# Causal masking without mask products: a fused maximum on VectorE and zeroed exponentials on GpSimd, with later sums and projections

## The chip, the cores and the metric

One core of a Trainium2 chip runs the whole program. The metric is the device time of one execution in microseconds (us); less is better. The core has five engines with a queue each: TensorE (PE in the profile), VectorE (DVE), ScalarE (ACT), GpSimd (POOL), and SyncE (SP), which issues DMAs. They meet only through semaphores.

## The reference, cut to what matters

The model looks up token vectors (16 sequences of 512, width 128), mixes them once with a low-rank attention, and then runs a block with routed experts and an MLP. The change is in the block's three attentions, 8 heads of width 16 over 512 tokens each. Spatial (S) and cross (C) attention see all keys, temporal (T) attention is causal:

```python
logits = jnp.einsum('bthd,bshd->bhts', q, k) * HD ** (-0.5)
causal = jnp.tril(jnp.ones((T, T), dtype=bool))
logits = jnp.where(causal, logits, -jnp.inf)
att = jax.nn.softmax(logits, axis=-1)
o = jnp.einsum('bhts,bshd->bthd', att, v).reshape(B, T, D)
```

## The kernel before, in words

There are three stages, one after the other: `embed_and_mix`, `attend`, `feed_forward`. The change touches `attend` alone, which computes for each of the 16 sequences three units, S, T and C.

A unit passes through PE twice. First the scores are computed with queries on the partitions, only to find each query's maximum: 32 tiles (8 heads x 4 blocks of 128 queries), `score` (line 1114), each reduced by VectorE in `reduce` (919). The negated maxima are split into three bf16 rows and stacked under the queries (`negate`, 927). Then the scores are computed again, keys on the partitions, with the maximum already subtracted: 32 tiles, `logits` (1129), each taken through Exp by ScalarE into `probs` (`exponential`, 1026). Four tiles make a group; `weigh` (1144) multiplies a group with the values and sums over the keys: 8 sums per unit, of which the first four belong to the first half of the heads. For T, only the causal part of a tile is computed, 128 to 512 columns, and each tile of both passes gets one more product of 128 columns that adds -1e30 above the diagonal: lines 1125 and 1140, `ident_bf` times `mask_row` or `mask_col`.

q, k and v come from fp32 projections into one PSUM bank, the desk (`project`, 1084). ScalarE keeps q and k; GpSimd splits them in bf16 parts (`split`, 841), SyncE stacks the parts by DMA (`stack`, 794).

The order is written out by hand. The loop runs over i, each with three slots of 32 tiles. In a slot, four units are at work (`units`, 731): `kn` is projected and split, `ka` is scored, `kb` is in its second pass (its first 24 tiles), `ko` ends (its last 8 tiles, the last sums, the merges and the output). Slot 0: kn = T, ka = S, kb = C, ko = T. Slot 1: kn = C, ka = T, kb = S, ko = C. Slot 2: kn = S, ka = C, kb = T, ko = S. At tile n, PE does score n, what falls due at n (the projections at PROJECT_AT, in desk order), logit n - 8, and a sum where n % 4 is 3. The others follow the same count: ScalarE keeps q and k at KEPT_AT, copies the second group of sums (`s_high`, `u_high`) at tile 12 and the first (`s_all`, `u_all`) at tile 28, and makes the reciprocal at 21 (a logarithm and an exponential); VectorE adds the value bias at VALUES_AT and shuffles the merged sums at SWAP_AT, 17 (`swap`, 962), after waiting for GpSimd's merge (line 870).

GpSimd's own queue in a slot (863): split q and k of `kn`, merge `s_all` (870) and `u_all` (871) of `ko`, an affine or a bias in some slots, the product with the reciprocal (889), and in slots 1 and 2 the affine for a later unit.

Two rings limit how far the engines run apart. There are three PSUM banks for scores, so score n waits until reduction n - 3 is done, and three for logits, so logit n waits for exponential n - 3. `probs` has two buffers, one group each, so the exponentials of group q wait for sum q - 2. The sums of all groups share one bank, so sum 0 waits for ScalarE's copy of the second group of the unit before, and sum 4 for the copy of the first.

## Time and profile before

| | us |
|---|---|
| median of 3 runs | 1764.1 |
| lowest and highest | 1762.8, 1768.21 |
| the profiled execution | 1757.12 |
| its span, first to last instruction | 1755.3 |
| busy: PE / VectorE / ScalarE / GpSimd | 1584.6 / 1277.1 / 1117.8 / 814.3 |

The attention stage runs from about 276 us to about 1600 us of the span. In its middle it is periodic: one repeat of three slots takes 78.28 us. All rows below are taken from one repeat: slot 2 from 781.47 us, slot 0 from 807.44, slot 1 from 833.25 to 859.75.

The profile lists for each group of instructions its busy time and the mean duration of one. Matmuls are pipelined, so the records of successive ones overlap; how much time one takes in PE's stream is read from the distance between starts. Vector and scalar instructions overlap a little too: where a row of the timeline merges several (x14), its length divided by their number gives the pace.

### The profile page before, as it was taken

The page shows a single profiled execution, that of the slowest core. Times are in us where ns is not written, and L with a number is a line of the kernel's source. Part 1 is how long each engine was busy: PE and PEld are TensorE (multiplying, and loading weights), DVE is VectorE, ACT ScalarE, POOL GpSimd, SP SyncE. Part 2 cuts the span into 40 slices and gives each one's busy share as a digit, 9 for nine tenths or more (in the row PEclk, how much of TensorE's full clock was granted, in tenths as well). Part 3 has the DMA queues.
Part 4 walks back from the last instruction along what each step waited for, and adds up shares of the span by engine and source line. Part 5 has one row for each costly group of instructions (what it writes and reads, how often), then busy time and mean ns, then how long its engine had stood idle before and what let it go on. Part 6 is the DMA issues. An engine that isn't in the chain of part 4 may idle for free. (4 is left out here: it accounts for less than half of the span.)

```text
span 1755.3 us, 37109 instructions
## 1 busy us (share of the span) xinstructions
PE 1584.6 (90%) x9638; PEld 727.3 (41%) x9638; DVE 1277.1 (73%) x3087; ACT 1117.8 (64%) x2185; POOL 814.3 (46%) x865
## 2 busy tenths in 40 slices
PE   3668956999999999999999999999999999865998
PEld 1217942334434344434444343444444443211675
DVE  6886857388787887878787887879788787452442
ACT  3324850747777778687777778777777878714333
POOL 7832443345545545545544544544554553222443
PEclk9858966989999999999999999999999999956999
DMA  1211125366446546546546545645645644020221
GB/s 51 72 48 33 47 59 75 45 81 80 66 61 81 71 55 86 71 54 78 74 59 72 81 61 71 79 58 67 82 64 61 88 58 56 1 37 26 61 66 54
DMA packets 132339, 109.25 MB, mean 62 GB/s; under 512 B 21825, under 2 KB 125249, under 8 KB 132289
## 3 DMA queue, kind: packets, MB, share of 16 engines
q1 hardware_dynamic: 130240, 104.44, 42.0%
q0 software_dynamic: 2048, 4.20, 0.9%
q8 instruction: 25, 0.41, 0.1%
q14 instruction: 26, 0.20, 0.1%
HBM read 19.26 MB, written 8.39 MB: 16 GB/s over the span
## 5 line engine op out<-in xcount | busy, mean ns | idle before, releaser
L1032 ACT ACTIVATE probs<-psum 128x512 f32<-128x512 f32 (+3 forms) x1536 | 738.9, 552 | 316.7 <-PE psum L1137 197.7
L924 DVE TENSOR_REDUCE mx_S<-psum 128x1 f32<-128x512 f32 x512 | 323.3, 684 | 51.5 <-PE psum L1122 49.7
L924 DVE TENSOR_REDUCE mx_C<-psum 128x1 f32<-128x512 f32 x512 | 317.6, 681 | 46.7 <-PE psum L1122 45.4
L924 DVE TENSOR_REDUCE mx_T<-psum 128x1 f32<-128x128 f32 (+3 forms) x512 | 243.5, 489 | 120.8 <-PE psum L1125 108.1
L852 POOL CAST parts_q<-f_q 128x512 bf16<-128x512 f32 x48 | 29.2, 609 | 439.5 <-ACT f_q L1023 439.5
L1122 PE MATMUL psum<-ks_C,qs_C 96*128 96x512 bf16 x512 | 202.9, 398 | 5.1 <-DMA ks_C<-parts_k 1.0
L1122 PE MATMUL psum<-ks_S,qs_S 96*128 96x512 bf16 x512 | 199.8, 396 | 6.4 <-DVE mx_S L924 5.2
L1137 PE MATMUL psum<-qs_C,ks_C 99*128 99x512 bf16 x512 | 194.4, 391 | 10.6 <-DMA qs_C<-ng_p 6.4
L1137 PE MATMUL psum<-qs_S,ks_S 99*128 99x512 bf16 x512 | 195.9, 384 | 1.4 <-DMA qs_S<-ng_p 0.7
L1137 PE MATMUL psum<-qs_T,ks_T 99*128 99x256 bf16 (+3 forms) x512 | 153.2, 302 | 7.0 <-ACT probs L1032 5.6
L1122 PE MATMUL psum<-ks_T,qs_T 96*128 96x128 bf16 (+3 forms) x512 | 157.1, 309 | 1.2 <-DVE mx_T L924 0.9
L1157 PE MATMUL psum<-probs,va_C 128*32 128x512 f32 x1024 | 138.2, 612 | 0.7
L1157 PE MATMUL psum<-probs,va_S 128*32 128x512 f32 x1024 | 136.4, 605 | 0.3
L1125 PE MATMUL psum<-mask_row,ident_bf 128*128 128x128 bf16 x512 | 114.3, 224 | 0.0
L1140 PE MATMUL psum<-mask_col,ident_bf 128*128 128x128 bf16 x512 | 112.0, 220 | 0.0
L1122 PEld LDWEIGHTS psum<-ks_C,qs_C 96*128 96x128 bf16 x512 | 49.8, 97 | 140.1 <-DVE mx_C L924 86.4
L870 POOL TENSOR_TENSOR s_all<-s_all,s_high 128x512 f32<-128x512 f32 x48 | 61.3, 1276 | 97.4 <-ACT u_high L1040 97.4
L1122 PEld LDWEIGHTS psum<-ks_S,qs_S 96*128 96x128 bf16 x512 | 49.9, 98 | 131.6 <-DVE mx_S L924 86.8
L1371 ACT ACTIVATE gT<-psum,b 128x512 f32<-128x512 f32 x64 | 44.0, 687 | 94.7 <-PE psum L1391 94.7
L1157 PE MATMUL psum<-probs,va_T 128*32 128x512 f32 (+3 forms) x1024 | 96.6, 449 | 0.0
L1122 PEld LDWEIGHTS psum<-ks_T,qs_T 96*128 96x128 bf16 x512 | 50.8, 99 | 106.2 <-DVE mx_T L924 79.6
L1137 PEld LDWEIGHTS psum<-qs_C,ks_C 99*128 99x128 bf16 x512 | 49.0, 98 | 79.3 <-ACT probs L1032 46.9
(188 smaller groups left out, 2722.3 us busy)
## 6 DMA issues: line engine op xcount, KB each, us to landing
qs_S<-parts_q SPq DMA_DIRECT2D x96, 128.0 KB, 4.4
ks_S<-parts_k SPq DMA_DIRECT2D x96, 128.0 KB, 6.8
qs_T<-parts_q SPq DMA_DIRECT2D x96, 128.0 KB, 4.4
ks_T<-parts_k SPq DMA_DIRECT2D x96, 128.0 KB, 6.6
qs_C<-parts_q SPq DMA_DIRECT2D x96, 128.0 KB, 4.4
ks_C<-parts_k SPq DMA_DIRECT2D x96, 128.0 KB, 6.7
w_in_S<-in_s_in SPq DMA_DIRECT2D x16, 257.0 KB, 2.7
w_in_T<-in_t_in SPq DMA_DIRECT2D x16, 257.0 KB, 2.7
```

The source lines that it names most:

```text
L852: nc.gpsimd.tensor_copy(parts[c][:, 0, :], f32[c][:]).then_inc(hi_done, 1)
L870: nc.gpsimd.tensor_tensor(s_all[:], s_all[:], s_high[:], ALU.add).then_inc(s_merged, 1)
L924: nc.vector.tensor_reduce(mx[kind][:, n:n + 1], psum[:, ring_place(kind, b, n, RL), 0:last_key], AX_X, ALU.max)\
L1032: nc.scalar.activation(probs[:, n // 4 % 2, n % 4, t0:T], psum[:, LOGITS + ring_place(kind, b, n, RC), t0:T], ACT.Exp, scale=SCALE).then_i ...
L1122: last = nc.tensor.matmul(psum[:, ring_place(kind, b, n, RL), 0:keys], qs[kind][0:RA, hd, P * tb:P * tb + P], ks[kind][0:RA, hd, 0:keys], ...
L1125: last = nc.tensor.matmul(psum[:, ring_place(kind, b, n, RL), P * tb:keys], ident_bf[:], mask_row[:], start=False, stop=True, skip_group_c ...
L1137: last = nc.tensor.matmul(psum[:, bank, t0:T], ks[kind][0:RB, hd, P * s:P * s + P], qs[kind][0:RB, hd, t0:T], start=True, stop=True)
L1140: last = nc.tensor.matmul(psum[:, bank, t0:t0 + P], ident_bf[:], mask_col[:], start=False, stop=True, skip_group_check=True)
L1157: last = nc.tensor.matmul(sums[32 * j:32 * j + 32, t0:T], va[kind][:, s, g, j, :], probs[:, q % 2, j, t0:T], start=(s == 0), stop=(kind == ...
L1371: nc.scalar.activation(gT[:, odd, f, :], psum[:, 1 + f, :], ACT.Gelu, bias=b1[:, f:f + 1])\
```

## The change

No mask products are made any more. In the first pass VectorE's reduction of a T tile becomes one fused instruction that adds a mask tile (`causal`, zeros with -1e30 in the last 128 columns above the diagonal, cut to the tile's width) and takes the maximum; it also writes the sum back to PSUM. In the second pass the logits stay unmasked, and GpSimd sets the exponentials above the diagonal to zero, once for each group of four tiles (`zero_future`, 4 x 128 columns, 8 per T unit). The causal sums wait for this cut and come two tiles later (`CAUSAL_WEIGH_AFTER` 9 instead of 7). `probs` gets a third buffer, for which the weights `s_outs` are laid into its last buffer during the start. Projections, keeping and the value bias come later: PROJECT_AT from (3, 7, 10) to (5, 8, 12), KEPT_AT from (4, 8) to (6, 9), VALUES_AT from 13 to 16. SWAP_AT (17), RECIP_AT (21) and the two copies (12 and 28) stay.

```diff
-PROJECT_AT = (3, 7, 10)
-KEPT_AT = (4, 8)
-WEIGH_AT = 3
-VALUES_AT = 13
+PROJECT_AT = (5, 8, 12)
+KEPT_AT = (6, 9)
+WEIGH_AFTER, CAUSAL_WEIGH_AFTER = 7, 9
+VALUES_AT = 16
-RL, RC = 3, 3
+RL, RC, RP = 3, 3, 3
@@ GpSimd
+                def zero_future(kind, b, q):
+
+                    if kind != "T" or not exists(b):
+                        return
+                    pool.wait_ge(exped, TILES * unit_no("T", b) + 4 * q + 4)
+                    pool.sem_inc(cut_seen, 1)
+                    t0 = first_key("T", 4 * q)
+                    diagonal = probs[:, group_place("T", b, q), :, t0:t0 + P]
+                    nc.gpsimd.affine_select(out=diagonal, in_=diagonal, compare_op=ALU.is_ge, fill=0.0, base=0,
+                                            pattern=[[0, 4], [1, P]], channel_multiplier=-1).then_inc(cut, 1)
                 def slot_program(i, slot):
-                    (kn, bn), _, _, (ko, bo) = units(i, slot)
-                    split(kn, bn)
+                    (kn, bn), _, (kb, bb), (ko, bo) = units(i, slot)
+                    zero_future(ko, bo, 5)
+                    zero_future(ko, bo, 6)
+                    zero_future(ko, bo, 7)
+                    split(kn, bn, 0)
+                    zero_future(kb, bb, 0)
+                    split(kn, bn, 1)
+                    zero_future(kb, bb, 1)
                     if exists(bo):
                         u = unit_no(ko, bo)
                         pool.wait_ge(high_out, u + 1)
                         pool.wait_ge(low_out, u + 1)
                         nc.gpsimd.tensor_tensor(s_all[:], s_all[:], s_high[:], ALU.add).then_inc(s_merged, 1)
                         nc.gpsimd.tensor_tensor(u_all[:], u_all[:], u_high[:], ALU.add).then_inc(u_merged, 1)
+                    zero_future(kb, bb, 2)
...
+                    zero_future(kb, bb, 3)
                     if exists(bo):
...
+                    zero_future(kb, bb, 4)
@@ VectorE
-                    last_key = P * (n % NB + 1) if kind == "T" else T
-                    nc.vector.tensor_reduce(mx[kind][:, n:n + 1], psum[:, ring_place(kind, b, n, RL), 0:last_key], AX_X, ALU.max)\
-                        .then_inc(reduced, 1)
+                    tile = psum[:, ring_place(kind, b, n, RL), :]
+                    if kind == "T":
+                        dve.sem_inc(scored_seen, 1)
+                        last_key = P * (n % NB + 1)
+                        nc.vector.tensor_tensor_reduce(tile[:, 0:last_key], tile[:, 0:last_key],
+                                                       causal[:, T - last_key:T], 1.0, NEG, ALU.add, ALU.max,
+                                                       mx[kind][:, n:n + 1]).then_inc(reduced, 1)
+                    else:
+                        nc.vector.tensor_reduce(mx[kind][:, n:n + 1], tile, AX_X, ALU.max).then_inc(reduced, 1)
@@ ScalarE
-                        at_least(act, summed, 8 * u + n // 4 - 1)
+                        at_least(act, summed, 8 * u + n // 4 - RP + 1)
@@ TensorE
-                    if kind == "T":
-                        last = nc.tensor.matmul(psum[:, ring_place(kind, b, n, RL), P * tb:keys], ident_bf[:], mask_row[:],
-                                                start=False, stop=True, skip_group_check=True)
...
-                    if kind == "T":
-                        last = nc.tensor.matmul(psum[:, bank, t0:t0 + P], ident_bf[:], mask_col[:],
-                                                start=False, stop=True, skip_group_check=True)
...
-                    pe.wait_ge(exped, TILES * u + 4 * q + 4)
+                    if kind == "T":
+                        pe.wait_ge(cut, 2 * NB * b + q + 1)
+                    else:
+                        pe.wait_ge(exped, TILES * u + 4 * q + 4)
...
-                        if n % 4 == WEIGH_AT:
-                            q = (n - LAG) // 4 - 1
-                            if q < 0 and exists(bo):
-                                weigh(ko, bo, q + 8)
-                            if q >= 0 and exists(bb):
-                                weigh(kb, bb, q)
+                        for kind, b, first in ((ko, bo, LAG - TILES), (kb, bb, LAG)):
+                            lag = CAUSAL_WEIGH_AFTER if kind == "T" else WEIGH_AFTER
+                            q, rest = divmod(n - first - lag, 4)
+                            if rest == 0 and 0 <= q < 2 * NB and exists(b):
+                                weigh(kind, b, q)
```

## Rows read from the trace of the kernel before

**Rows 1.** The page, part 1: busy time, share of the span, instructions.
```profile
PE 1584.6 (90%) x9638; PEld 727.3 (41%) x9638; DVE 1277.1 (73%) x3087; ACT 1117.8 (64%) x2185; POOL 814.3 (46%) x865
```

**Rows 2.** Slots 2, 0, 1: stretch, length, busy of each engine, clock, DMA.
```profile
781.47:807.44 25.97, 25.09 (x170) 10.60 (x166) 22.35 (x43) 18.68 (x40) 12.81 (x13) 1.00 0.52 62
807.44:833.25 25.81, 25.29 (x157) 10.15 (x154) 23.04 (x43) 19.48 (x40) 12.77 (x13) 1.00 0.56 72
833.25:859.75 26.50, 26.48 (x185) 11.64 (x181) 18.29 (x44) 21.35 (x40) 13.96 (x14) 1.00 0.57 75
```

**Rows 3.** Groups of instructions by form: busy us, mean ns, idle before.
```profile
L1125 PE MATMUL psum<-mask_row,ident_bf 128*128 128x128 bf16 x512 | 114.3, 224 | 0.0
L1140 PE MATMUL psum<-mask_col,ident_bf 128*128 128x128 bf16 x512 | 112.0, 220 | 0.0
L924 DVE TENSOR_REDUCE mx_T<-psum 128x1 f32<-128x512 f32 x128 | 87.8, 686 | 9.0 <-PE psum L1125 9.0
L996 DVE TENSOR_TENSOR X<-X,psum 128x512 f32 x13 | 8.8, 679 | 0.0
```

**Rows 4.** Timeline, slot 2, PE: start us, length us, engine, line, operation.
```profile
802.89 0.38 PE L1137 MATMUL psum<-qs_T,ks_T 99*128 99x512 bf16 x1
803.11 0.22 PE L1140 MATMUL psum<-mask_col,ident_bf 128*128 128x128 bf16 x1
803.17 0.38 PE L1122 MATMUL psum<-ks_C,qs_C 96*128 96x512 bf16 x1
```

**Rows 5.** Timeline, tile 3 of slot 2: projection, sum 5, reductions 2 and 3.
```profile
783.61 1.12 PE L1105 MATMUL psum<-xn,w_in_S 128*128 128x512 f32 x2 [0.34 <-DVE ng L931]
784.60 1.27 DVE L924 TENSOR_REDUCE mx_C<-psum 128x1 f32<-128x512 f32 x2
784.88 1.07 PE L1157 MATMUL psum<-probs,va_S 128*32 128x512 f32 x8
```

**Rows 6.** Timeline, slot 2, VectorE: the shuffle and the reductions behind it.
```profile
798.08 0.75 DVE L968 STREAM_SHUFFLE s_right<-s_all 128x512 f32<-128x512 f32 x1
798.72 8.47 DVE L924 TENSOR_REDUCE mx_C<-psum 128x1 f32<-128x512 f32 x14
```

**Rows 7.** Timeline, slot 2, GpSimd: q's split begins, the first merge.
```profile
786.47 0.61 POOL L852 CAST parts_q<-f_q 128x512 bf16<-128x512 f32 x1 [8.33 <-ACT f_q L1023]
794.76 1.28 POOL L870 TENSOR_TENSOR s_all<-s_all,s_high 128x512 f32<-128x512 f32 x1 [0.62 <-ACT u_high L1040]
```

**Rows 8.** Timeline, slot 0: GpSimd, exponential 7, shuffle, score 21.
```profile
812.13 0.61 POOL L852 CAST parts_q<-f_q 128x512 bf16<-128x512 f32 x1 [7.44 <-ACT f_q L1023]
...
819.75 1.28 POOL L870 TENSOR_TENSOR s_all<-s_all,s_high 128x512 f32<-128x512 f32 x1
...
814.17 0.28 ACT L1032 ACTIVATE probs<-psum 128x128 f32<-128x128 f32 x1 [1.09 <-PE psum L1140]
...
822.41 0.73 DVE L968 STREAM_SHUFFLE s_right<-s_all 128x512 f32<-128x512 f32 x1
...
824.05 0.38 PE L1122 MATMUL psum<-ks_S,qs_S 96*128 96x512 bf16 x1
```

**Rows 9.** One line's instructions: the selection of 128 columns on GpSimd.
```profile
L908 POOL TENSOR_SCALAR_AFFINE_SELECT mask_col<-mask_col x1: 292/292/292, 265.4 to 265.4; 128x128 bf16<-128x128 bf16 x1
```

**Rows 10.** Timeline, slot 1: ScalarE behind the reciprocal, merge, shuffle.
```profile
852.68 3.51 ACT L1032 ACTIVATE probs<-psum 128x512 f32<-128x512 f32 x7
...
845.74 1.27 POOL L870 TENSOR_TENSOR s_all<-s_all,s_high 128x512 f32<-128x512 f32 x1 [0.46 <-ACT u_high L1040]
...
848.61 0.74 DVE L968 STREAM_SHUFFLE s_right<-s_all 128x512 f32<-128x512 f32 x1
```

**Rows 11.** Timeline, end of slot 2: causal sum 3 and the last logit.
```profile
803.75 0.42 PE L1157 MATMUL psum<-probs,va_T 128*32 128x128 f32 x8
...
806.11 0.34 PE L1137 MATMUL psum<-qs_T,ks_T 99*128 99x384 bf16 x1 [0.27 <-ACT probs L1032]
```

**Rows 12.** Groups of instructions: ScalarE's one reading of an accumulator.
```profile
L538 ACT ACTIVATION_READ_ACCUMULATOR rex<-rl,rsc 16x1 f32 x1 | 0.2, 185 | 0.0
```

More of the change, by code:

```diff
@@ L104, in ring_place, with group_place @@
     return (TILES * u + n) % ring
+def group_place(kind, b, q):
+    return ring_place(kind, b, 4 * q, 4 * RP) // 4
 def at_least(eng, sem, value):
@@ L701, in attend @@
         exped = sem("exped2")
+        cut, cut_seen = sem("cut"), sem("cut_seen")
+        masks_made, scored_seen = sem("masks_made"), sem("scored_seen")
         summed = sem("summed2")
@@ L839, in affine, with split @@
                     nc.gpsimd.tensor_tensor(to[:], scaled[:], s, ALU.add).then_inc(affine_done, 1)
-                def split(kind, b):
+                def split(kind, b, *which):
                     if not exists(b):
                         return
-                    for c in range(2):
+                    for c in which:
                         n = 2 * unit_no(kind, b) + c
@@ L898, in _ @@
                 affine(xn, 0, 0, "xn")
[L899 to L900 removed]
+                nc.gpsimd.memset(causal[:], 0.0)
                 for k in KINDS:
@@ L1136, in logits @@
                     bank = LOGITS + ring_place(kind, b, n, RC)
-                    last = nc.tensor.matmul(psum[:, bank, t0:T], ks[kind][0:RB, hd, P * s:P * s + P],
-                                            qs[kind][0:RB, hd, t0:T], start=True, stop=True)
-                    if kind == "T":
-                        last = nc.tensor.matmul(psum[:, bank, t0:t0 + P], ident_bf[:], mask_col[:],
-                                                start=False, stop=True, skip_group_check=True)
-                    last.then_inc(logits_in, 1)
+                    nc.tensor.matmul(psum[:, bank, t0:T], ks[kind][0:RB, hd, P * s:P * s + P],
+                                     qs[kind][0:RB, hd, t0:T], start=True, stop=True).then_inc(logits_in, 1)
                 def weigh(kind, b, q):
```

33 lines of the change are left out of this document (13 added, 20 removed).

## The prediction

> **What bounds the kernel now.** The page first [rows 1]: TensorE (PE) is busy 90% of the span, VectorE 73%, ScalarE 64%, GpSimd 46%. The change lies in the attention stage, so I cut one repeat of that stage into its three slots, from score to score: 25.97 us for slot 2 (scores of C, exponentials of T), 25.81 for slot 0 (scores of S), 26.50 for slot 1 (scores of T) [rows 2]. One repeat is 78.28 us; there are 16 units of each kind, and I count 14 full repeats, since the first and last overlap with filling and draining. Times below that start near 0 are counted from the slot's start: 781.47, 807.44 and 833.25.
>
> Busy time of a matmul is not its price. In the timeline a mask product stands at 803.11 and the next score at 803.17 [rows 4]: it takes 0.057 us of PE's stream (128 columns at the full clock, which rows 2 show as 1.00), although its record says 0.22 [rows 3]. Who waits for whom differs by slot. Slot 1: PE's stream is nearly gapless, and behind it ScalarE runs seven exponentials in 3.51 us without a gap from 852.68 [rows 10]. Slot 2: from 798.72 VectorE makes 14 reductions in 8.47 us without a gap [rows 6], so VectorE sets the pace there, not PE. Slot 0: PE, with a little of both.
>
> **What goes.** All 1024 mask products [rows 3]: 64 per repeat, 32 in slot 1, 24 in slot 2, 8 in slot 0, 3.65 us per repeat, 57 us in all if every one were on the path. That is the ceiling of the gain. The Trainium skill ("Trainium Kernel Development and Optimization", Performance Expectations) warns that busy time of matmuls is a bad metric; whoever took it would hope for 226 us here, and rows 4 side with the warning.
>
> **Slot 1, -1.35 us.** Up to tile 20 PE leads: 20 x 0.057 = 1.15. From tile 20 to 27 ScalarE is continuous (eight exponentials at 0.49, a logarithm and an exponential), so masks gone there give nothing. Tiles 28 to 31: 0.2 again. The fused add-and-maximum has no row. Nearest: a two-input VectorE operation from PSUM over 512 elements, 0.68, against 0.69 for the reduction it replaces [rows 3]. I take no extra cost, since VectorE is busy only 18.3 of 26.5 us here [rows 2]; from below nothing is to be gained either. One mask tile loaded once, less start-up copies, costs nothing I can count.
>
> **What is moved, and the queue it is moved in.** The weight is in GpSimd's queue. Today: q is split as soon as ScalarE has kept it, then k, then the two merges, and VectorE's shuffle (SWAP_AT, tile 17, not moved) waits for the first merge. Slot 2: split from 5.0, first merge 13.29 to 14.57, shuffle at 16.61: 2.0 us of slack [rows 6, 7]. Slot 0: split from 4.69, merge ends 13.59, shuffle 14.97: 1.4 us of slack [rows 8]. The change puts work and waits ahead of that merge.
>
> The cut of one group (4 x 128 elements): the row shows 0.29 us for 128 [rows 9]. Below bound 0.29; above 1.28, a two-input operation of 512 [rows 7]; I take 0.61, the one-input cast of 512 [rows 7], as the cut reads one input. By the Trainium skill (GPSIMD Engine Reference, 4.1 Engine selection) one-input work runs at about line rate, an estimate of 0.43 us for 512; the sum below would be 0.5 us less per repeat, no row can tell.
>
> *Slot 0, +1.85 us.* GpSimd must first cut groups 5, 6, 7 of the T unit that ends. Group 7 needs the exponential of this slot's tile 7, which ends at 7.01 today [rows 8]. Afterwards one projection (tile 8) has left these eight tiles and one causal sum (tile 1) has come in; the negation still holds score 5 until about 3.9 (it needs reduction 2, which starts behind the negation at 3.1 [rows 5]), then projection 0.96, causal sum 0.85 (between 0.42 for 128 columns and 1.07 for 512 [rows 5, 11]), two tiles: about 7.2. Cut 7 ends at about 8.1. Only then does q's split start, 3.4 us later than today. From split to end of merge is 8.90 us [rows 8]: 17.0. VectorE would be at the shuffle near 15 and stands until 17.1. Behind it in its queue are the reductions 18 and on; PE's score 21 waits for reduction 18, whose end comes at 17.1 + 0.63 + 0.69 = 18.5. Today score 21 stands at 824.05, that is 16.61 [rows 8]. From there to the slot's end PE needs 9.2 us with hardly a wait, and no mask product among it. So +1.85. The later causal sum 7 (tile 13, one tile behind ScalarE's copy at tile 12, which waits for it) stalls exponentials by some 0.9 us, but just ahead of this wait, which swallows it, as it swallows the 8 masks.
>
> *Slot 2, +0.95 us.* Good: q's projection leaves tile 3, where it waits for the negation (0.34 us idle) and is followed at once by a sum of 1.07 [rows 5]; VectorE starves less. Bad: q is kept about 1.6 us later (tile 6), split 6.8 to 10.6; cut 0 needs the exponential of tile 11, about 11.7, and ends 12.3; k's split 12.35 to 16.15; cut 1 to 16.75; merge to 18.1. VectorE would be at the shuffle at 16.2, so it stands 1.9 us and reduction 18 starts at 18.8, against 17.25 today [rows 6]. From there VectorE sets the pace. At the end another wait comes: ScalarE's copies of the first group (tile 28) now wait for a causal sum at tile 29. Today from that sum (803.75) to the logit that needs the freed bank (806.11) it is 2.4 us [rows 11]; two tiles later and with less PE work between, PE waits 1.2 instead of 0.45. VectorE's pace puts score 29 at 24.3, last logit 26.8, slot end 26.95 instead of 25.97. This takes in the 24 masks: VectorE and ScalarE, not PE, stand last.
>
> *Hidden:* slot 1 has no cuts; its merge ends at 15.0 instead of 13.76 (q kept later), shuffle 15.36 today [rows 10], some 0.75 us of standing VectorE, which has room and whose next waiter, score 21, is a sum away. k's stacking DMAs are issued 3.5 us later in slots 0 and 2, 1.7 in slot 1; they land one to four microseconds ahead of the next slot's first score. If that cover went, the first score would wait by the remainder. Three exponential buffers loosen only a wait that rarely ends last. The weights in the third buffer are used only before the loop.
>
> **The sum.** Per repeat -1.35 + 1.85 + 0.95 = +1.45; x 14 = +20. The profiled execution took 1757.1 (span 1755.3 and 1.8 around it), 0.4% under the median of 1764.1. 1757.1 + 20.3 = 1777.4, or 1.2% more; on the median, **1784 us**. With the cut at 0.29: 0.3 less in slot 0 and 0.6 in slot 2 (two cuts), +7. At 1.28: 0.65 and 1.3 more, +48, 1812. Slot 1's term by itself: 0 to -1.8, that is +19 or -6 us. Own range 1770 to 1807.
>
> **Rivals.** *A, the merge is in time* and the shuffle never stands: it holds if the cuts and their waits put the merge back by less than the 1.4 to 2.0 us of slack. For it: GpSimd is idle half the time [rows 2]. Against: it is an in-order queue and cut 7 waits for a fixed tile. Then slot 1 -1.35, slot 0 -0.25 (masks 0.46 and the negation's wait 0.65 gone, ScalarE's copy 0.85 later), slot 2 -1.0: -2.6 x 14 = -36, 1728 (1715 to 1748).
> *B, half of it:* only slot 0's merge is late (slot 2's group 0 is ready sooner than I reckon). +1.85 - 1.35 - 1.0 = -0.5, -7 us: 1757 (1750 to 1769).
> *C, slower, the fused operation is dear.* Place: VectorE in slot 1, 32 times. It decides from (25.15 - 18.3 - 0.75) / 32 = 0.19 us above the reduction. At one more pass over its mean of 320 columns (0.33 us) VectorE's 18.3 becomes 29 and the slot 29.7, +3.2 instead of -1.35: +64 more, 1848 on top of the forecast (1810 to 1850). Against it: the two-input row at 0.68. By the Trainium skill (VectorE: DVE Perf Modes, Two Vector instructions with no wait between them) an operation that also writes its accumulator is two instructions, which no row of VectorE shows here. ScalarE's one reading of an accumulator took 0.185 us [rows 12], right at that threshold.
>
> **Chances.** Forecast (late merge, slower) 0.60; A 0.22; B 0.11; C 0.07. About 0.3% (5 us) is what a measurement of this kernel can tell from no change. B is split between faster (0.05) and same (0.06), 0.02 of the forecast lies within 0.3%: faster 0.27, same 0.08, slower 0.65. The range 1735 to 1812 leaves out the faster part of A and C, less than 0.2.
>
> **What would show it.** Slots of about 27.6, 25.2 and 27.0 us; VectorE idle some 2 us before the shuffle in slots 0 and 2, released by GpSimd's merge; q's split starting near 8 in slot 0; PE's score 21 waiting for VectorE. If the shuffle has no idle time before it, A holds. If VectorE is gapless in slot 1 and the fused operation is above 0.85 us at 512, C. If the clock falls below 1.00 in the middle, none of these sums holds.

## The result, and the profile after

The changed kernel takes **1867.7 us** (median of 4 runs, 1867.0 to 1871.3) against 1764.4 for the kernel before on the same chip: ratio 1.058, 95% interval 1.055 to 1.060, 103 us slower. The prediction had 1784 (1735 to 1812): slower, as forecast, but by five times as much; the forecast is 84 us short. The profiled execution's span is 1865.1 us.

The page of the changed kernel: busy time, the clock granted to TensorE (PE) in 40 slices of the span, and the queue by which instructions are fetched (packets, MB, share):

```profile
PE 1595.0 (86%) x8614; PEld 665.9 (36%) x8614; DVE 1298.3 (70%) x3598; ACT 1113.9 (60%) x2185; POOL 892.2 (48%) x991
...
PEclk9859956889999989898989999898989899977999
...
q14 instruction: 87, 0.71, 0.1%
```

PE's 1024 mask products are gone from the count [rows 1], yet its busy time rose by 10 us. The middle of the clock line is no longer even, and 87 packets of instructions were fetched where the kernel before fetched 26. Both will matter. One repeat in its three slots, to be laid beside rows 2 (stretch, length, busy of PE, PEld, VectorE, ScalarE, GpSimd, clock, DMA), and five stretches inside it:

```profile
914.84:943.87 29.03, 24.18 (x137) 8.92 (x134) 22.83 (x43) 18.12 (x41) 15.77 (x18) 0.94 0.47 56
943.87:974.36 30.49, 29.15 (x154) 10.29 (x154) 23.02 (x43) 20.13 (x42) 14.69 (x17) 0.89 0.49 62
974.36:1000.17 25.81, 25.09 (x154) 9.52 (x150) 19.30 (x76) 20.97 (x40) 13.94 (x14) 1.00 0.58 78
931.60:935.00 3.40, 0.61 (x6) 0.34 (x10) 2.02 (x6) 1.13 (x3) 3.04 (x3) 0.99 1.18 124
935.00:938.40 3.40, 3.40 (x16) 0.95 (x8) 2.80 (x5) 0.99 (x5) 0.60 (x2) 0.50 0.24 22
941.80:945.20 3.40, 2.00 (x12) 0.73 (x14) 1.58 (x3) 3.25 (x8) 2.68 (x3) 1.00 0.01 2
945.20:948.60 3.40, 3.16 (x14) 0.74 (x6) 3.07 (x9) 0.95 (x4) 0.19 (x1) 0.50 0.01 2
948.60:952.00 3.40, 3.35 (x12) 0.96 (x12) 1.79 (x3) 1.00 (x3) 0.44 (x1) 0.50 0.14 18
```

Slot by slot, medians over the repeats in the middle of the stage against the forecast:

| per repeat, us | before | forecast | changed | at half clock |
|---|---|---|---|---|
| slot 1 | 26.50 | 25.15 | 25.78 | 0 |
| slot 2 | 25.96 | 26.95 | 29.03 | 3.98 |
| slot 0 | 25.81 | 27.66 | 30.52 | 6.26 |
| repeat | 78.3 | 79.7 | 85.3 | 10.2 |

The repeat grew by 7.0 us, and 14 of these are 98 of the 103 us: the loss is all in the periodic middle, as the sum assumed. The last column (a mean, the others are medians) is what the sum excluded. In the repeat above two stretches ran at a clock of 0.50 (1.2 instead of 2.4 GHz), both after PE had stood: one of some 3.4 us in slot 2, before which PE was busy 0.61 of 3.40 us, and one of some 6.8 us early in slot 0, before which it was busy 2.00 of 3.40 us.

**Slot 2, the chain that was forecast.** Timeline, GpSimd, VectorE and PE (idle time and its releaser in brackets):

```profile
926.56 0.64 POOL L876 TENSOR_SCALAR_AFFINE_SELECT probs<-probs 128x512 f32<-128x512 f32 x1 [0.89 <-ACT probs L1060]
...
931.57 1.26 POOL L892 TENSOR_TENSOR s_all<-s_all,s_high 128x512 f32<-128x512 f32 x1
...
932.98 0.06 DVE L158 MEMSET scrap<- 1x1 f32 x1 [2.32 <-POOL s_all L892]
...
933.65 2.46 DVE L952 TENSOR_REDUCE mx_C<-psum 128x1 f32<-128x512 f32 x4
...
934.38 0.39 PE L1150 MATMUL psum<-ks_C,qs_C 96*128 96x512 bf16 x1 [3.15 <-DVE mx_C L952]
```

From the slot's start at 914.84, the merge ends at 17.99 (forecast 18.1), VectorE has stood 2.32 us for it (1.9), reduction 18 starts at 18.81 (18.8), and PE's score 21 follows after 3.15 us of nothing. Before, the same merge ended at 14.57 and nobody waited [rows 6, 7].

**The end of slot 2**, ScalarE's copy of the first group and the last logit:

```profile
941.58 0.69 ACT L1093 ACTIVATE s_all<-psum,high 128x512 f32<-128x512 f32 x1 [0.58 <-PE psum L1180]
...
943.28 0.34 PE L1161 MATMUL psum<-qs_T,ks_T 99*128 99x384 bf16 x1 [1.14 <-ACT probs L1060]
```

ScalarE stands 0.58 us for the sum that now comes a tile behind the copy; the logit waits 1.14 us (forecast 1.2; before 0.27 [rows 11]).

**Slot 0, another story than the forecast.** Timeline, VectorE's first reductions; GpSimd's cut 7 and the merge; VectorE at the shuffle:

```profile
945.23 1.29 DVE L952 TENSOR_REDUCE mx_S<-psum 128x1 f32<-128x512 f32 x2 [1.86 <-PE psum L1150]
...
953.50 0.63 POOL L876 TENSOR_SCALAR_AFFINE_SELECT probs<-probs 128x512 f32<-128x512 f32 x1 [4.45 <-ACT probs L1060]
...
961.71 1.27 POOL L892 TENSOR_TENSOR s_all<-s_all,s_high 128x512 f32<-128x512 f32 x1
...
961.79 0.69 DVE L952 TENSOR_REDUCE mx_S<-psum 128x1 f32<-128x512 f32 x1 [2.11 <-PE psum L1150]
...
963.68 0.75 DVE L995 STREAM_SHUFFLE s_right<-s_all 128x512 f32<-128x512 f32 x1
```

Cut 7 ends at 10.3 from the slot's start, not 8.1, and the merge at 19.1, not 17.0. Yet the shuffle at 19.8 does not stand: VectorE came even later than the merge, having itself waited 2.11 us for a score. And the first reduction starts 1.36 us behind the score it reads (943.87), where before the delay was 0.43 us. The row names PE, but PE's score had long been done; nothing on this row explains it.

**The groups on VectorE and GpSimd by form** (busy us, mean ns, idle before):

```profile
L948 DVE CUSTOM_DVE_ANT_0 psum<-psum,causal 128x512 f32<-128x512 f32 x128 | 92.3, 721 | 5.3 <-PE psum L1150 4.1
L948 DVE DVE_READ_ACCUMULATOR2_ANT mx_T<- 128x1 f32 x512 | 72.7, 142 | 0.0
...
L876 POOL TENSOR_SCALAR_AFFINE_SELECT probs<-probs 128x512 f32<-128x512 f32 x128 | 81.2, 634 | 225.4 <-ACT probs L1060 225.4
```

The cut is 0.634 us (taken: 0.61). The fused operation is 721 ns against 686 for the reduction [rows 3], and it is two instructions, with a second of 142 ns: 0.86 us together, at the line of 0.85 that the forecast drew for rival C, though VectorE is far from gapless in slot 1 (19.30 of 25.81). The Trainium skill ("VectorE: DVE Perf Modes", Two Vector instructions with no wait between them) has an operation that also writes out its accumulator as two instructions; the second row above agrees.

### The profile page after: what moved, and what is told of

Read it like the earlier page. It is cut to its first block and busy times, and to the rows that moved or that the text cites. A ratio compares the mean times of both kernels' runs of the same rounds, so it can differ in the third digit from the quotient of the medians.

```text
span 1865.1 us, 36441 instructions
## 1 busy us (share of the span) xinstructions
PE 1595.0 (86%) x8614; PEld 665.9 (36%) x8614; DVE 1298.3 (70%) x3598; ACT 1113.9 (60%) x2185; POOL 892.2 (48%) x991
## 5 line engine op out<-in xcount | busy, mean ns | idle before, releaser
L948 DVE CUSTOM_DVE_ANT_0 psum<-psum,causal 128x128 f32<-128x128 f32 (+3 forms) x512 | 246.2, 509 | 95.9 <-PE psum L1150 92.2
L1150 PE MATMUL psum<-ks_C,qs_C 96*128 96x512 bf16 x512 | 212.2, 426 | 50.7 <-DVE mx_C L952 49.5
L1150 PE MATMUL psum<-ks_S,qs_S 96*128 96x512 bf16 x512 | 210.0, 422 | 20.3 <-DVE mx_S L952 16.1
L876 POOL TENSOR_SCALAR_AFFINE_SELECT probs<-probs 128x512 f32<-128x512 f32 x128 | 81.2, 634 | 225.4 <-ACT probs L1060 225.4
L1161 PE MATMUL psum<-qs_T,ks_T 99*128 99x256 bf16 (+3 forms) x512 | 168.6, 333 | 22.5 <-ACT probs L1060 22.3
L1180 PE MATMUL psum<-probs,va_T 128*32 128x512 f32 (+3 forms) x1024 | 116.4, 532 | 1.0 <-POOL probs L876 0.7
L1161 PEld LDWEIGHTS psum<-qs_T,ks_T 99*128 99x128 bf16 x512 | 54.4, 107 | 70.3 <-ACT probs L1060 45.5
```

The source lines that it names most:

```text
L876: nc.gpsimd.affine_select(out=diagonal, in_=diagonal, compare_op=ALU.is_ge, fill=0.0, base=0, pattern=[[0, 4], [1, P]], channel_multiplier ...
L948: nc.vector.tensor_tensor_reduce(tile[:, 0:last_key], tile[:, 0:last_key], causal[:, T - last_key:T], 1.0, NEG, ALU.add, ALU.max, mx[kind] ...
L1150: nc.tensor.matmul(psum[:, ring_place(kind, b, n, RL), 0:keys], qs[kind][0:RA, hd, P * tb:P * tb + P], ks[kind][0:RA, hd, 0:keys], start=T ...
L1161: nc.tensor.matmul(psum[:, bank, t0:T], ks[kind][0:RB, hd, P * s:P * s + P], qs[kind][0:RB, hd, t0:T], start=True, stop=True).then_inc(log ...
L1180: last = nc.tensor.matmul(sums[32 * j:32 * j + 32, t0:T], va[kind][:, s, g, j, :], probs[:, group_place(kind, b, q), j, t0:T], start=(s == 0),
```

## The experiments

Four theories were tried: the forecast's late merge (*shuffle*); *clock*, that the stalls cost twice because PE is then slow; *moves*, that later projections, values and sums cost what I had called hidden or swallowed; *code*, that VectorE waits for its own instructions. Each ratio is to the kernel before as measured beside that kernel on the same chip, and differences below are (ratio - 1) x 1764 us; slots are medians, in the order 1, 2, 0; the last column is the mean time at half clock in slots 2 and 0.

| kernel | ratio, 95% interval | us | slots 1 / 2 / 0 | half clock |
|---|---|---|---|---|
| changed | 1.0577 [1.0552, 1.0602] | +102 | 25.78 / 29.03 / 30.52 | 3.98, 6.26 |
| no_masks | 0.9853 [0.9837, 0.9870] | -26 | 25.26 / 25.57 / 25.70 | 0, 0 |
| only_later | 1.0159 [1.0127, 1.0192] | +28 | 26.44 / 26.64 / 27.04 | 0, 0 |
| fused_only | 1.0000 [0.9987, 1.0012] | 0 | 25.45 / 25.97 / 26.92 | 0, 0.57 |
| no_cuts | 1.0287 [1.0270, 1.0304] | +51 | 25.79 / 25.56 / 30.58 | 0, 3.41 |
| shuffle_late | 1.0246 [1.0217, 1.0275] | +43 | 25.79 / 25.32 / 30.52 | 0, 3.41 |
| copies_late | 1.0556 [1.0527, 1.0584] | +98 | 25.78 / 28.52 / 32.13 | 5.69, 4.55 |
| both_late | 1.0218 [1.0196, 1.0241] | +38 | 25.78 / 23.88 / 32.23 | 0, 6.83 |
| filled | 1.0412 [1.0383, 1.0442] | +73 | 25.78 / 27.68 / 29.11 | 0, 3.41 |
| padded | 1.0123 [1.0099, 1.0147] | +22 | 26.72 / 25.97 / 26.94 | 0, 0.85 |
| early_again | 1.0321 [1.0299, 1.0344] | +57 | 25.45 / 28.55 / 28.83 | 2.84, 1.99 |
| after_plain | 1.0462 [1.0444, 1.0479] | +81 | 25.41 / 29.03 / 28.34 | 4.84, 1.71 |
| three_undone | 1.0050 [1.0033, 1.0067] | +9 | 25.25 / 25.94 / 27.02 | 0, 0.56 |
| late_sums | 1.0023 [1.0014, 1.0033] | +4 | 25.26 / 25.62 / 27.05 | 0.01, 1.41 |
| max_unmasked | 0.9894 [0.9872, 0.9916] | -19 | 25.26 / 25.97 / 25.82 | 0, 0 |
| reordered | 1.0027 [1.0013, 1.0042] | +5 | 25.25 / 25.62 / 27.03 | 0.02, 1.12 |
| sums_copies | 0.9828 [0.9812, 0.9844] | -30 | 25.26 / 24.18 / 26.62 | 0, 0 |
| reordered_copies | 0.9839 [0.9823, 0.9855] | -28 | 25.25 / 24.18 / 26.62 | 0, 0 |
| with_masks | 0.9974 [0.9965, 0.9984] | -5 | 26.50 / 24.56 / 26.89 | 0, 0 |

### What the mask products were worth

**no_masks**, the kernel before without either product:

```diff
-                        last = nc.tensor.matmul(... ident_bf[:], mask_row[:], ...)
-                        last = nc.tensor.matmul(... ident_bf[:], mask_col[:], ...)
```

> The kernel before with all 1024 mask products left out and nothing in their place, so the causal mask is missing: it measures what their absence is worth when nothing is paid for it. By the slot sums: slot 1 saves 1.35 us, slot 0 0.4, slot 2 0.2 to 0.5 (VectorE sets its pace), 28 to 32 us in all: 1732 to 1738. If TensorE were the bound everywhere, 57 us: 1707. Theory W allows a third outcome: less TensorE work, more gaps, a clock below 1.00 in places, and then no gain at all.

26 us, not 57 (and a little under the 28 to 32 expected): slot 1 gains 1.24 (forecast 1.35), slots 2 and 0 gain 0.39 and 0.11, since other engines stand last there. This is all that the change could win as the order of work stood.

### The moves alone

**only_later**, the kernel before with nothing but the new places of projections, keeping and values:

```diff
-PROJECT_AT = (3, 7, 10)
-KEPT_AT = (4, 8)
-VALUES_AT = 13
+PROJECT_AT = (5, 8, 12)
+KEPT_AT = (6, 9)
+VALUES_AT = 16
```

> The kernel before with the later projections, keeping and value bias alone; mask products, sums and everything else as before. Theory W (the loss comes from waits that the cuts and the two tiles later causal sums create, and from the halved TensorE clock that follows them): GpSimd's merge comes 1.7 us later in its slot, about as much as its slack of 1.4 to 2.0 us, and the projection no longer waits for the negation: 1752 to 1770 us. Rival P (the moved projections are themselves the harm): above 1800 us.

28 us, with the clock at 1.00 throughout the three slots; at 1790.6 us it lies between the two expectations, and neither held. Slot 0 of a repeat of only_later starts at 906.16; timeline, PE and VectorE around tile 16:

```profile
918.77 0.39 PE L1137 MATMUL psum<-qs_C,ks_C 99*128 99x512 bf16 x1 [0.30 <-ACT probs L1032]
919.20 1.06 PE L1157 MATMUL psum<-probs,va_C 128*32 128x512 f32 x8
920.20 0.39 PE L1122 MATMUL psum<-ks_S,qs_S 96*128 96x512 bf16 x1
...
920.63 0.69 DVE L924 TENSOR_REDUCE mx_S<-psum 128x1 f32<-128x512 f32 x1 [1.66 <-PE psum L1122]
921.24 0.75 DVE L952 TENSOR_TENSOR va_T<-psum,w_in_T 128x256 f32<-128x256 f32 x2
...
922.51 0.74 DVE L968 STREAM_SHUFFLE s_right<-s_all 128x512 f32<-128x512 f32 x1
...
923.90 0.39 PE L1122 MATMUL psum<-ks_S,qs_S 96*128 96x512 bf16 x1 [0.24 <-DVE mx_S L924]
```

The work is the same, but the values (tile 16) now lie against the shuffle (tile 17). VectorE idles 1.66 us and then has some 1.4 us of other work with a single reduction between, just when three score banks must be emptied. PE's waits for reductions agree: 1.1 us in slot 0 and 1.0 us in slot 2, and no wait of over 0.15 us in either slot of the kernel before. No run moved the values alone, so that they, and not the projections, are the harm is read from these rows and not shown.

**early_again**, the changed kernel with the three old constants:

```diff
-PROJECT_AT = (5, 8, 12)
-KEPT_AT = (6, 9)
+PROJECT_AT = (3, 7, 10)
+KEPT_AT = (4, 8)
...
-VALUES_AT = 16
+VALUES_AT = 13
```

> The changed kernel with the old places of projections, keeping and value bias, (3, 7, 10), (4, 8), 13. Alone, their move cost 26 us. Theory A (the costs add up): 1835 to 1850. Theory W (in the changed kernel GpSimd's split then starts 1.7 us sooner and the merge is nearly in time in slot 2, so a half-clock stretch goes with it): 1790 to 1825. Rival: no difference, 1860 or more, since GpSimd waits for the cuts anyway.

45 us less than the changed kernel, more than half of it in slot 0, where the half clock falls from 6.26 to 1.99 us. The moves cost more inside the changed kernel (45) than alone (28).

### The late merge

**shuffle_late**, and **no_cuts** (`zero_future` returns at once, sums wait for ScalarE alone, and the exponentials above the diagonal stay in them):

```diff
-SWAP_AT, RECIP_AT = 17, 21
+SWAP_AT, RECIP_AT = 21, 24
```

```diff
-                    if kind == "T":
-                        pe.wait_ge(cut, 2 * NB * b + q + 1)
-                    else:
-                        pe.wait_ge(exped, TILES * u + 4 * q + 4)
+                    pe.wait_ge(exped, TILES * u + 4 * q + 4)
```

> The changed kernel with VectorE's shuffle at tile 21 instead of 17 and the reciprocal at 24 instead of 21: only where the wait for GpSimd's merge stands in VectorE's queue. Theory W: the 2.3 us of standing VectorE in slot 2 go, with them the half-clock stretch behind it; the copies' waits stay: 1800 to 1840. Rival S (the later sums and ScalarE's copies are the whole loss): 1860 to 1868, unchanged.

> The changed kernel without GpSimd's cuts (the causal sums wait for the exponentials only, still two tiles late), so the second pass is unmasked: it leaves the exponentials above the diagonal in. Theory W: the shuffle's wait of 2.3 us in slot 2 is gone or under 0.3, but ScalarE's two copies still wait for the later sums; the clock keeps one or two half stretches a repeat: 1780 to 1830, 40 to 85 us under the changed kernel. Rival G (GpSimd's cuts are the whole loss): about 1730. Rival S (the later sums are the whole loss): 1860 as the changed kernel.

Either takes slot 2 back from 29.03 to about 25.4 and saves 58 and 51 us: the late merge is real and costs 3.5 to 3.7 us there. The forecast had given it 1.95, from -1.0 with the merge in time (rival A) to +0.95. Slot 0 does not move by a tenth (30.52 and 30.58): in the changed kernel the late merge does not set its end. Its time at half clock falls from 6.26 to 3.41 us without making it shorter, so that time is no measure of what the clock costs there.

### The clock by itself

**filled** adds useless work to the changed kernel: ten products of 512 columns into a free bank, five ahead of each of scores 20 and 21 in slot 2, where PE would stand.

```diff
+                        if ko == "S" and ... and n in (20, 21):
...
+                            for _ in range(5):
+                                nc.tensor.matmul(desk, ks[kb][0:RA, 0, 0:P], qs[kb][0:RA, 0, :], start=True, stop=True)
```

> The changed kernel with ten useless products of 512 columns (2.1 us) in slot 2, tiles 20 and 21, just ahead of score 21, where TensorE stands idle 3.1 us for VectorE's shuffle; they write to the free desk bank and nobody reads them. It adds work and takes away no wait, so only the clock can make it faster. Theory W: the half-clock stretch that follows this wait goes; 15 to 40 us under the changed kernel: 1828 to 1853. If the clock costs nothing by itself: 1868 or more.

More work, 29 us less. Slots 2 and 0 of a repeat (this slot 0 is longer than the median of 29.11), and the timeline of the wait:

```profile
900.99:928.72 27.73, 24.98 (x147) 9.54 (x144) 22.56 (x43) 18.21 (x41) 15.85 (x18) 1.00 0.48 58
928.72:959.92 31.20, 27.96 (x154) 9.99 (x154) 23.53 (x43) 20.01 (x42) 14.66 (x16) 0.95 0.47 60
```

```profile
918.31 1.24 PE L1212 MATMUL psum<-qs_T,ks_T 96*128 96x512 bf16 x5
...
919.14 0.06 DVE L158 MEMSET scrap<- 1x1 f32 x1 [2.33 <-POOL s_all L892]
...
920.54 0.39 PE L1150 MATMUL psum<-ks_C,qs_C 96*128 96x512 bf16 x1 [0.99 <-DVE mx_C L952]
```

VectorE waits for the merge exactly as before the filling (2.33 and 2.32 us), and score 21 starts at 19.55 from the slot's start (19.54 without the filling). But PE kept its clock, and from there to the slot's end it takes 8.2 us instead of 9.5. So 1.3 us of slot 2's loss is the clock and nothing else. Slot 0, which begins in better order, is 1.4 us shorter by the median, but a third of the repeats have it at 31, as the one above; on the mean it gains 0.6. The Trainium skill ("TensorE: Matmul & The Clock Gate", Part 1) has the clock follow how busy PE has been of late, with two levels; the stretches here show those two, and the lower one right behind a wait of 3 us in the midst of dense work.

### VectorE's code

**fused_only** puts the fused operation into the kernel before in place of the score masks (the logits keep theirs). **padded** is the kernel before with two empty semaphore instructions ahead of each reduction of T. **after_plain** is the changed kernel with plain reductions, whose maximum is taken over the whole diagonal block: a bound from above, which serves the softmax as well. The edits of padded and after_plain:

```diff
+                    if kind == "T":
+                        dve.sem_inc(pad, 1)
+                        dve.sem_inc(pad, 1)
```

```diff
-                        nc.vector.tensor_tensor_reduce(tile[:, 0:last_key], tile[:, 0:last_key], causal[:, T - last_key:T], ...)
+                    nc.vector.tensor_reduce(mx[kind][:, n:n + 1], tile[:, 0:last_key], AX_X, ALU.max).then_inc(reduced, 1)
```

> The kernel before with only the score masks replaced by VectorE's fused add and maximum (512 mask products gone, 512 kept, all sums and tiles in their old place). Theory W: slot 1 saves about 1 us and nothing else moves: 1745 to 1755. Rival F (the fused operation with its separate reading of the accumulator, 0.142 us each, makes VectorE the bound of slot 1): 1770 or more.

> The kernel before with two empty semaphore increments on VectorE ahead of each reduction of T: no work and no wait, only 64 more instructions in VectorE's loop. Theory L (the fused operation, three instructions where there was one, makes VectorE's loop outgrow what it holds of its code, and the jump back at the start of slot 0 then waits about 1 us for code): code fetches appear on the instruction queue in the steady part (5 a repeat, as in the changed kernel), the first reduction of slot 0 starts 1.3 to 1.5 us after its score instead of 0.43, and the time grows by 10 to 20 us: 1774 to 1784. Rival F (the delay comes from the fused operation itself): 1762 to 1768.

> The changed kernel with the plain reduction for T instead of the fused one (the maximum is then taken over the whole diagonal block, an upper bound of the masked one). Theory, code fetches of VectorE's loop cost 1.1 to 1.75 us of a repeat: instruction packets fall from 87 to about 26, the first reduction of slot 0 starts 0.4 us behind its score instead of 1.4, slot 0 gets 1.1 to 1.7 us shorter and slot 1 0.2 to 0.5, so 17 to 30 us less than the changed kernel, 1838 to 1851. Rival, in the changed kernel the fetch hides in waits for other engines: within 5 us of 1867. Third, the repair also ends a stretch of half clock, then 40 us or more less.

fused_only wins 1.05 us in slot 1 and loses 1.11 in slot 0, where no instruction was changed; its sum of zero was in neither expectation. padded, whose additions do nothing at all, loses the same 1.1 us in slot 0 (and 0.2 in slot 1), so the fused operation itself is not needed for it. In both, and in every other kernel with the fused operation, the page shows 87 packets of instructions, and 25 or 26 in all the others. Padded, slot 0 from 904.95: its first reduction, and the DMA queues from 904 to 912:

```profile
906.38 1.29 DVE L928 TENSOR_REDUCE mx_S<-psum 128x1 f32<-128x512 f32 x2 [1.68 <-PE psum L1126]
```

```profile
q1 hardware_dynamic: 144, 0.02, 1.6%
q14 instruction: 3, 0.02, 1.1%
```

The reduction starts 1.43 us behind its score, and three instruction packets arrive in these 8 us; the kernel before has none in the same place. The 61 packets more are 0.51 MB, some 8 KB each, and in the middle of the stage they come five to a repeat. The traces of fused_only and of padded record 330 instructions of VectorE in a repeat, waits included, that of the kernel before 266. So the loop body on VectorE has become too long to stay where it runs from, part of it is fetched again in each repeat, and the first reduction of slot 0, at the loop's start, waits for it. That it is VectorE's code that comes in the packets I infer from who waits; no packet names its engine. In both_late (below) the same reduction stands 1.82 us for nothing that the profile shows, and PE then stands for the reductions; timeline, slot 0 from 907.53:

```profile
910.37 1.29 DVE L952 TENSOR_REDUCE mx_S<-psum 128x1 f32<-128x512 f32 x2 [1.82 <-issue]
...
914.27 0.61 PE L1150 MATMUL psum<-ks_S,qs_S 96*128 96x512 bf16 x1 [2.10 <-DVE mx_S L952]
```

("issue" marks time for which the profile shows no wait.) From 913.35 on the clock is 0.50 for 6.83 us. By these rows the fetch is also behind that half clock; no run takes only the fetch out of both_late.

after_plain has 25 packets, a delay of 0.43 us, and is 20 us below the changed kernel.

### The later sums

**late_sums** is the kernel without masks plus the two tiles of delay of the causal sums and the third buffer: no cuts, plain reductions, old places. **three_undone** is the changed kernel less the three causes found so far (shuffle at 21, old places, plain reductions). Both carry the edits of early_again and after_plain, late_sums that of no_cuts too, three_undone that of shuffle_late.

> Mask products gone, causal sums two tiles later, third buffer; no cuts (exponentials above the diagonal stay in the sums), plain reductions for T, old places of projections, keeping and values. It should be the kernel without masks (1738) plus what the two tiles cost. Theory, ScalarE's copies stand behind the later sums: slot 0 27.0 to 27.5 instead of 25.70, slot 2 as without masks, 1755 to 1765. Rival, the later sums are free with three buffers: 1736 to 1743.

> The changed kernel with plain reductions for T (no fused operation; maximum over the whole diagonal block), the old places of projections, keeping and values, and the shuffle at tile 21 with the reciprocal at 24. What is left of the change: cuts on GpSimd, causal sums two tiles later, third buffer, no mask products. Theory, the causes add up (1867 less 61 for the shuffle, 44 for the places, 20 for the code fetches, with some overlap, and no half clock left): 1745 to 1770. Rival, the late sums and cuts cost by themselves: 1775 to 1800, with slot 0 above 28 us.

The delay alone turns -26 into +4: **30 us**, the whole gain of the masks. three_undone adds the cuts (with the shuffle at 21), for only 5 us more. Slot 0 of late_sums from 886.68; ScalarE and PE:

```profile
899.35 0.69 ACT L1060 ACTIVATE s_high<-psum,low 128x512 f32<-128x512 f32 x1 [1.19 <-PE psum L1170]
...
898.77 0.43 PE L1170 MATMUL psum<-probs,va_T 128*32 128x128 f32 x8
...
901.16 0.39 PE L1154 MATMUL psum<-qs_C,ks_C 99*128 99x512 bf16 x1 [1.21 <-ACT probs L1053]
```

ScalarE reaches the copy of tile 12 and stands 1.19 us, because the sum it copies comes at tile 13. The exponentials of tile 12 and on are behind it in the queue, their banks stay full, and PE's logit 15 waits 1.21 us. The same happens at tile 28 of slot 2 (PE waits 1.14 us), and behind it slot 0 begins with a stretch at half clock in 5 of 12 repeats.

**copies_late** and **both_late** move the copies two tiles back for T, in the changed kernel and in shuffle_late; **sums_copies** and **reordered_copies** do so in late_sums and in reordered, a version of the changed kernel with plain reductions, old places and the cuts placed so that both splits are hardly held up:

```diff
-                        if n == GROUP_2_AT and exists(bo):
+                        if n == GROUP_2_AT + (2 if ko == "T" else 0) and exists(bo):
-                        if n == GROUP_1_AT and exists(bb):
+                        if n == GROUP_1_AT + (2 if kb == "T" else 0) and exists(bb):
```

The order of the cuts in reordered:

```diff
-                    zero_future(ko, bo, 7)
                     split(kn, bn, 0)
-                    zero_future(kb, bb, 0)
+                    zero_future(ko, bo, 7)
                     split(kn, bn, 1)
-                    zero_future(kb, bb, 1)
+                    zero_future(kb, bb, 0)
...
+                    zero_future(kb, bb, 1)
                     zero_future(kb, bb, 2)
```

> The changed kernel with ScalarE's copies of the sums two tiles later where the unit is causal (tile 30 for the first group, 14 for the second), so that they follow the causal sum as they did before. Theory W: TensorE's idle time at the end of slot 2 shrinks from about 1.5 us to 0.5, and the two half-clock stretches at the start of slot 0 go or become one: 1800 to 1835; the wait at the shuffle stays. Rival G (GpSimd's order is the whole loss): 1860 to 1868.

> The changed kernel with both: shuffle at 21, reciprocal at 24, causal copies two tiles later. Theory W: no half-clock stretch is left in the repeat, and the time comes to the kernel before less part of the mask products: 1725 to 1760. If waits and clock are not the cause, it stays above 1820.

> late_sums (no mask products, causal sums two tiles later, no cuts, so exponentials above the diagonal stay in the sums; plain reductions, old places) with ScalarE's copies of the sums of T two tiles later as well, 14 and 30. Theory, the two tiles cost only because the copies at 12 and 28 wait at the head of ScalarE's queue for a sum that now comes a tile behind them: slot 0 falls from 27.05 towards 25.7 and no half clock is left, 1738 to 1748. Rival, the copies merely move the wait to the sums behind them, which need the bank the copies free (as the copies did in the changed kernel): slot 0 stays at 27.0 or above, 1757 to 1775.

> A version meant to keep the gain: no mask products, plain reductions over the unmasked scores, the old places of the projections, GpSimd's cuts put where nobody waits (cut 7 between the splits of q and k in slot 0, cut 0 behind both splits, cut 1 behind the merges in slot 2), causal sums two tiles late as in the change. By the theory of waits and clock the merge comes at 14.5 to 15 us in both slots, before the shuffle; ScalarE's copies still wait for the later sums: 1740 to 1775. If the later sums alone carry most of the loss: above 1790.

> reordered (the changed kernel with plain reductions, old places and GpSimd's cuts in another order; 1770) with ScalarE's copies of the sums of T at tiles 14 and 30. Same two theories: copies alone stood behind the sums, slot 0 falls from 27.0 to about 25.8, 1745 to 1755, which would be a version with GpSimd's cuts that beats the kernel before; or the wait moves, 1765 to 1790.

In the changed kernel the copies' new places are worth 4 us: slot 2 gains 0.5 and slot 0 loses 1.6. That is what the rival named for copies_late, not the 1800 to 1835 of the theory, and both_late (1803.3) missed its 1725 to 1760: no half clock was to be left, and 6.83 us are, behind the late first reduction shown above. So the waits that these two kernels take away were not the whole cause.

With moves and fused operation gone the same edit is worth 34 us on late_sums and 33 on reordered, 10 to 16 us more than the expectations' better ends. PE's waits for exponentials, 1.14 us in slot 2 and 1.21 in slot 0, are gone, and no half clock is left. I had put the gain into slot 0, and most of it came in slot 2 (25.62 to 24.18). The two slots must be read together, since the two tiles of delay also carry one causal sum over their border; the kernel before (slot 0 from 807.44) and reordered_copies (from 874.22), PE:

```profile
806.44 1.07 PE L1157 MATMUL psum<-probs,va_T 128*32 128x512 f32 x8
```

```profile
875.72 1.07 PE L1174 MATMUL psum<-probs,va_T 128*32 128x512 f32 x8
```

Slots 2 and 0 together take 51.27 us in no_masks, 52.67 in late_sums (and the half clock on top, 0.6 on the mean) and 50.80 in sums_copies. Copies moved without the later sums were not run. reordered_copies, slots 2, 0 and 1, and ScalarE's copy in slot 0, which no longer waits:

```profile
850.00:874.22 24.22, 22.83 (x137) 8.60 (x134) 21.18 (x42) 17.69 (x39) 14.49 (x17) 1.00 0.57 66
874.22:900.80 26.58, 25.77 (x154) 9.84 (x154) 23.96 (x45) 20.53 (x43) 15.91 (x18) 1.00 0.52 70
900.80:926.05 25.25, 24.87 (x153) 9.53 (x150) 18.00 (x44) 21.22 (x40) 13.92 (x14) 1.00 0.59 79
```

```profile
885.99 0.68 ACT L1061 ACTIVATE s_high<-psum,low 128x512 f32<-128x512 f32 x1
```

At 1728.7 us against 1757.6 beside it, this beats both kernels. **max_unmasked**, the kernel before with a single statement deleted, the score products' (so that the maximum is over the whole diagonal block), beats it too, by 19 us:

```diff
-                        last = nc.tensor.matmul(psum[:, ring_place(kind, b, n, RL), P * tb:keys], ident_bf[:], mask_row[:], ...)
```

> The kernel before without the score masks and with nothing in their place: the subtracted value is then the maximum over the whole diagonal block, an upper bound of the causal maximum, which softmax allows; the logits' masks stay. 512 mask products less, VectorE unchanged. With no masks at all 26 us were saved; 32 of the 64 products a repeat go here, all in slot 1: slot 1 saves 1.05 us as with the fused operation, and slot 0 loses nothing: 1746 to 1752. Rival: 1764, if slot 1 gives its gain back to the next slot.

**with_masks** asks whose gain the 28 us are: reordered_copies with all mask products and no cuts.

```diff
+                    if kind == "T":
+                        last = nc.tensor.matmul(... ident_bf[:], mask_row[:], ...)
...
+                    if kind == "T":
+                        last = nc.tensor.matmul(... ident_bf[:], mask_col[:], ...)
```

> reordered_copies (1729) with all 1024 mask products made again and no cuts on GpSimd: that is the kernel before plus the causal sums and ScalarE's copies of T two tiles later and the third buffer of exponentials, nothing else. Theory, the mask products cost what they cost in the kernel before, 1.7 us of a repeat (26 us), in slot 1 above all: 1748 to 1760, slot 1 at 26.5. Rival, the gain of reordered_copies was in the later sums and copies, and the masks' products are hidden: 1725 to 1735. Third: with the products two tiles of delay are worth nothing, 1760 to 1770.

The better order is worth 5 us by itself; the absence of the mask products, cuts included, 24. So the idea of the change holds in part: zeroed exponentials, with a plain maximum over the whole diagonal block, get most of what the masks cost, and the schedule lost it. The fused maximum gets nothing: fused_only stands 19 us above max_unmasked, which differs from it by the plain reduction alone.

## Why the prediction was wrong

In short: the terms put at nothing were not nothing (the moved work, the later causal sums, VectorE's longer code, the clock), and the largest term, slot 0's, rested on a wait that did not set that slot's end.

*What goes.* Right. Ceiling 57, real worth 26, slot 1 by 1.24 against 1.35 (no_masks).

*Slot 1, -1.35.* Measured -0.72. "I take no extra cost" for the fused operation was wrong by 0.2 to 0.4 us: 25.45 in fused_only against 25.26 in max_unmasked, 25.78 in the changed kernel against 25.41 in after_plain. The moved work makes up the rest, 25.78 against 25.45 in early_again. The two instructions of the fused operation are 0.16 us dearer than the reduction on the mean of the four widths (509 + 142 against 489 ns). That lies under the 0.19 from which rival C decides, so C did not happen, but a threshold read from VectorE's idle time is no guarantee of cost zero below it.

*The cut at 0.61.* Right: 0.634.

*Slot 2, +0.95.* The mechanism was right up to score 21: cuts, splits and merge came within 0.3 us of their forecast times, and VectorE stood 2.3 us instead of 1.9. The term measured +3.07. What failed is "from there VectorE sets the pace": PE had stood 3.15 us, came back at half clock, and set the pace instead. filled puts 1.3 us of it on the clock. Some 0.7 us behind score 21 I have not taken apart.

*Slot 0, +1.85.* Measured +4.71, and the step was wrong, not only its size: cut 7 and the merge are late, but taking them out changes nothing. The slot is long for three reasons that the forecast set at nothing: the moves (1.2 us alone), the code fetch (1.1 alone) and the later sums (1.35 alone, with the sum that crosses the border). They add up to 3.7; the other 1.0 is not taken apart. Half clock is part of it, but shuffle_late has half as much of it in this slot and the same length.

*The direction.* Right, but by luck: it hung on the term of slot 0. With the forecast's own value for a merge that does not matter in slot 0, -0.25 instead of +1.85, its sum is -1.35 - 0.25 + 0.95 = -0.65 a repeat, -9 us: faster.

*Hidden.* "Projections and values hidden" failed: 28 us alone, 45 within the changed kernel. I had checked that the moved pieces have cover where they land for the readers of their results (the splits, the next slot's scores), and not what they stand next to on VectorE. The later causal sum, "which this wait swallows", failed with it: there was no such wait in slot 0 to swallow it, and it cost 30 us by itself.

*The condition at the end.* "If the clock falls below 1.00 in the middle, none of these sums holds" is what came true. It should have been a rival with a price: the forecast itself had PE's score 21 coming some 2 us late in slots 0 and 2, and the page of before shows the clock at 0.5 to 0.8 in single slices at both ends of the kernel, where PE stands.

**The account.** Built up from before: masks gone -26, later sums +30, cuts with a late shuffle +5, together +9 (three_undone). From there the shuffle back at 17, the moved work and the fused operation add 93. Taken from the changed kernel one at a time they give 58, 45 and 20, together 123: they overlap by 30. Each, when removed, also takes 3.7 to 6.8 us of half clock out of the repeat, which is the likely reason, not a shown one. How the 93 us divide among the three is thus not a fixed number, and with the order of removal it would come out differently.

## What to carry to other kernels

When an operation is moved or deferred by a tile or two, look at every in-order queue for what now stands in front of its consumer: here copies that waited at the head of ScalarE's queue for sums two tiles late cost 30 us, the whole gain, and shifting them by the same two tiles gave 33 back. A forecast that has TensorE standing for 2 to 3 us in the midst of dense work should price the slow stretch that follows, as a term of its own. And an unrolled loop can grow too long: VectorE's did between 266 and 330 recorded instructions a repeat. Watch the instruction queue's packets on the page when instructions are added, even empty ones.

## What the runs showed of the hardware

- TensorE's clock falls to 0.50 in the middle of a busy kernel: after 0.61 us busy of 3.40, and after 2.00 of 3.40 with no single wait above 1.14 us. Ten useless products of 512 columns ahead of a wait kept it at 1.00 and made the kernel 29 us faster.
- The kernel before runs with 26 packets of instruction fetches in all; with 64 empty instructions more in a repeat there are 87, and the first reduction of slot 0 starts 1.4 to 1.7 us behind its score instead of 0.43, 22 us in all (padded). The profile puts this wait down to the engine whose semaphore came last, TensorE, or, in both_late, to nothing it shows.
- The fused add-and-maximum with an accumulator took 721 ns at 128x512 from PSUM, and a further instruction of 142 ns; GpSimd's selection over 4 x 128 fp32 columns took 634 ns, against 292 for 128 bf16 columns [rows 9].
